# Head maxima and their reciprocals by VectorE's 32x32 block transposes instead of TensorE transposes

## The reference

```python
c = jax.lax.stop_gradient(jnp.max(log_x.real, axis=-1, keepdims=True))
x = jnp.exp(log_x - c + 2).real.reshape(Bsz, L, n * d)
y = jnp.matmul(x, C) + jnp.matmul(u, D)
```

## Time and profile before

| | |
|---|---|
| runs of the kernel before | 208.19, 209.32, 211.12 us; median 209.32 |
| span of the profiled execution | 206.2 us (the page gives no other time of that execution) |
| busy: PE, PE weight loads, DVE, ACT, POOL | 181.0, 163.3, 143.2, 116.5, 97.5 us |
| mean granted clock of PE | 0.991 |

### The profile page before, as it was taken

The page is one execution under the profiler, slowest core; times in us unless marked ns, Lnnn a source line. Parts: engine busy times, 40 slices in busy tenths (PEclk is TensorE's granted clock), DMA queues, the critical chain, the costliest instruction groups (busy, mean ns, idle before and its releaser), DMA issues. The chain is left out here.

```text
span 206.2 us, 4072 instructions
## 1 busy us (share of the span) xinstructions
PE 181.0 (88%) x1407; PEld 163.3 (79%) x1407; DVE 143.2 (69%) x411; ACT 116.5 (56%) x317; POOL 97.5 (47%) x144
## 2 busy tenths in 40 slices
PE   0498999999999999999694999988979979996993
PEld 0276789999899987887594898987969969995891
DVE  1859956753444434669587685995977959569994
ACT  2037986554433355454444577847759577693771
POOL 0116644999200002239576184672843917656441
PEclk9999999999999999999999699999999999999999
DMA  5991000000000000000000000010100100010012
GB/s 137 399 423 62 3 0 5 2 0 3 0 0 3 0 0 2 3 0 0 0 3 2 0 3 0 0 51 5 51 0 3 52 0 27 27 51 2 3 52 102
DMA packets 2566, 7.60 MB, mean 37 GB/s; under 512 B 309, under 2 KB 1122, under 8 KB 2290
## 3 DMA queue, kind: packets, MB, share of 16 engines
q1 hardware_dynamic: 2258, 7.15, 9.1%
q10 hardware_dynamic: 288, 0.20, 0.4%
HBM read 5.25 MB, written 2.10 MB: 36 GB/s over the span
## 5 line engine op out<-in xcount | busy, mean ns | idle before, releaser
L421 POOL TENSOR_TENSOR hid_p<-hid_f,hid_p 128x256 fp32r<-128x256 f32 x56 | 40.2, 734 | 35.8 <-ACT hid_p L566 27.6
L564 ACT ACTIVATE hid_f<-bank,pa 128x256 f32<-128x256 f32 x64 | 30.3, 478 | 22.6 <-PE bank L1091 22.6
L1091 PE MATMUL bank<-xaT_p,fc_p 128*128 128x256 f32 x192 | 35.7, 297 | 0.8 <-ACT hid_f L564 0.7
L1111 PE MATMUL bank<-hid_p,out_hi 128*128 128x256 f32 x128 | 33.6, 288 | 0.6 <-POOL hid_p L421 0.5
L473 ACT ACTIVATE X<-bank 128x128 f32<-128x128 f32 x64 | 17.6, 279 | 23.3 <-PE bank L935 23.1
L1091 PEld LDWEIGHTS bank<-xaT_p,fc_p 128*128 128x128 f32 x192 | 27.3, 191 | 3.4 <-issue 2.0
L932 PE MATMUL bank<-uT,pa 128*128 128x128 f32 x128 | 25.1, 280 | 0.1
L843 DVE TENSOR_SCALAR xp<-h,mv,rstd 128x128 f32<-128x128 f32 x32 | 22.5, 762 | 3.3 <-POOL rstd L439 3.3
L1111 PEld LDWEIGHTS bank<-hid_p,out_hi 128*128 128x128 f32 x128 | 23.8, 188 | 1.2 <-POOL hid_p L421 0.9
L935 PE MATMUL bank<-X,pa 128*128 128x128 f32 x120 | 23.2, 275 | 0.0
L566 ACT ACTIVATE hid_p<-bank,pa 128x256 fp32r<-128x256 f32 x48 | 23.0, 478 | 0.0
(11 more groups left out here) (123 smaller groups left out, 384.4 us busy)
## 6 DMA issues: line engine op xcount, KB each, us to landing
fc_w<-in_fc SPq DMA_DIRECT2D x2, 2048.0 KB, 11.2
out<-res SPq DMA_DIRECT2D x7, 256.0 KB, 2.0
pb<-in_pack_b SPq DMA_DIRECT2D x1, 320.0 KB, 4.2
pa<-in_pack_a SPq DMA_DIRECT2D x1, 279.0 KB, 3.5
out<-res SPq DMA_DIRECT2D x2, 128.0 KB, 1.7
conv_w<-in_conv ACTq DMA_DIRECT2D x1, 128.0 KB, 3.4
pc<-in_pack_c ACTq DMA_DIRECT2D x1, 66.5 KB, 3.8
rowsel<-in_rows SPq DMA_DIRECT2D x1, 64.0 KB, 3.8
```

The costliest lines, as they stand in the source:

```text
L421: nc.gpsimd.tensor_tensor(hid_p[1][:, half, c, :], hid_f[:, m % HID_SLOTS, :], hid_p[0][:, half, c, :].bitcast(F32), ALU.subtract).then_in ...
L564: full = nc.scalar.activation(hid_f[:, m % HID_SLOTS, :], src, ACT.Gelu, bias=bias)
L1091: last = mm(bank[5 + n % 2][:, 0:HALF], fc1_p[w][:, e * HID + c * P:e * HID + (c + 1) * P], xaT_p[m][:, b % 2, half, :], start=(k == 0), s ...
L1111: last = mm(out_bank(b, half)[:, half * HALF:(half + 1) * HALF], out_p[w][:, e, c * CH:(c + 1) * CH], hid_p[m][:, half, c, :], start=(c == ...
```

## The change

The maxima come from X itself: a reduce which transposes each 32x32 block (32 states of a quadrant of partitions by 32 chunks) as it reads, so that chunk k is on a partition of the same quadrant and the reduce runs over 32 states. As a head has 64 states, in two quadrants, PE swaps the quadrants of each pair by one matmul with a permutation matrix, and DVE takes the larger of its own and the swapped value (peak). Reciprocals follow, and two block transposes of a broadcast spread them back to the states' partitions in banks 0 and 1. The factor e squared moves into the product xh. The transposes of X and of r_s on PE, ACT's four copies, the spreading matmuls, the sel matrix with its load and its cast on POOL go. On DVE peak, reciprocal and block transposes stand where xh stands, behind the small rows L801; only the reduces stay at the old place.

```diff
-PC_COLS = dict(ident=P, iota=1, tile=NQ)
+PC_COLS = dict(ident=P, iota=1, swap=P)
...
-        amax = sb("amax", [P, 2, NQ, NH])
-        rcp = sb("rcp", [P, 2, NQ * NH])
-        r_s = sb("r_s", [P, 2, NS, NQ * NH])
-        r_T = sb("r_T", [NS * NQ * NH, 2, L], F32R)
+        amax = sb("amax", [P, 2, NP, T])
+        peak = sb("peak", [P, NP, T])
+        rcp = sb("rcp", [P, NP, T])
...
-        bank_rt = bank[4][0:NS * NQ * NH, 0:P]
+        bank_sw = bank[4][:, 0:NP * T]
...
-                sp.dma_start(sel_f[:], sel).then_inc(ld_sel, 16)
...
-                pool.wait_ge(ld_sel, 16)
-                nc.gpsimd.tensor_copy(sel_r[:], sel_f[:]).then_inc(sel_ready, 1)
...
-                        b = j + 3
-                        if n == 2 and b < NB:
-                            act.wait_ge(rt_done, b + 1)
-                            if b >= 2:
-                                act.wait_ge(R_done, 2 * (b - 1))
-
-                            for q in range(NQ):
-                                mask = pc[0:NS * NQ * NH, PC["tile"]][:, q:q + 1]
-                                last = nc.scalar.activation(r_T[:, b % 2, q * P:(q + 1) * P], bank_rt, ACT.Copy,
-                                                            scale=mask)
-                            last.then_inc(rT_ready, 1)
...
                     b = j + 3
                     if b < NB:
+                        g, bb = divmod(b, GB)
+                        dve.wait_ge(x2_ready[g], T)
+                        if b >= 2:
+                            dve.wait_ge(swap_done, b - 1)
                         for a in range(NP):
-                            dve.wait_ge(xt_done, 2 * b + a + 1)
-                            last = nc.vector.tensor_reduce(
-                                amax[:, b % 2, :, 2 * a:2 * a + 2],
-                                bank[a][:].rearrange("p (q n d) -> p q n d", q=NQ, n=2), AX.X, ALU.max,
-                                apply_absolute_value=True)
+                            last = nc.vector.tensor_reduce(amax[:, b % 2, a, :], X[:, g, a * GB + bb, :, :], AX.X, ALU.max,
+                                                           apply_absolute_value=True, apply_transpose=True)
                         last.then_inc(amax_ready, 1)
-                        dve.wait_ge(amax_ready, b + 1)
-
-                        chained(nc.vector.reciprocal(rcp[:, b % 2, :],
-                                                     amax[:, b % 2, :, :].rearrange("p q n -> p (q n)")))
-                        if b >= 2:
-                            dve.wait_ge(rt_done, b - 1)
-                        hi = r_s[:, b % 2, 0, :]
-                        chained(nc.vector.tensor_scalar(hi.bitcast(F32R), rcp[:, b % 2, :], E2, None, ALU.mult))
-                        nc.vector.scalar_tensor_tensor(out=r_s[:, b % 2, 1, :], in0=rcp[:, b % 2, :], scalar=E2,
-                                                       in1=hi, op0=ALU.mult, op1=ALU.subtract).then_inc(rs_ready, 1)
...
                         if b == 0:
                             dve.wait_ge(fc1_split, NE)
+                        dve.wait_ge(amax_ready, b + 1)
+                        dve.wait_ge(swap_done, b + 1)
+                        nc.vector.tensor_tensor(peak[:], amax[:, b % 2], bank_sw.rearrange("p (a i) -> p a i", a=NP),
+                                                ALU.max).then_inc(peak_ready, 1)
+                        dve.wait_ge(peak_ready, b + 1)
+                        chained(nc.vector.reciprocal(rcp[:], peak[:]))
                         for a in range(NP):
-                            dve.wait_ge(R_done, 2 * b + a + 1)
-                            if b >= 2:
-                                dve.wait_ge(y_done, b - 1)
-                            nc.vector.tensor_tensor(xh[:, b % 2, a, :],
-                                                    X[:, g, a * GB + bb, :, :].rearrange("p i k -> p (i k)"),
-                                                    bank[a][:], ALU.mult).then_inc(xh_ready, 1)
+                            last = nc.vector.transpose(bank[a][:].rearrange("p (i k) -> p i k", k=NCH),
+                                                       rcp[:, a, :].unsqueeze(2).broadcast_to([P, T, NCH]))
+                        chained(last)
+                        if b >= 2:
+                            dve.wait_ge(y_done, b - 1)
+                        for a in range(NP):
+                            nc.vector.scalar_tensor_tensor(
+                                out=xh[:, b % 2, a, :], in0=X[:, g, a * GB + bb, :, :].rearrange("p i k -> p (i k)"),
+                                scalar=E2, in1=bank[a][:], op0=ALU.mult, op1=ALU.mult).then_inc(xh_ready, 1)
...
                         if e == FUSED_FRONT:
                             pe.wait_ge(x2_ready[0], T)
-                            pe.wait_ge(rT_ready, 1)
+                            pe.wait_ge(peak_ready, 1)
...
-                def transpose_r(b):
-                    pe.wait_ge(rs_ready, b + 1)
+                def swap_quadrants(b):
+                    pe.wait_ge(amax_ready, b + 1)
...
-                    nc.tensor.transpose(bank_rt, r_s[:, b % 2, :, :].rearrange("p s n -> p (s n)"),
-                                        ident).then_inc(rt_done, 1)
-
-                def spread_r(b):
...
+                    mm(bank_sw, pc[:, PC["swap"]], amax[:, b % 2].rearrange("p a i -> p (a i)"), start=True,
+                       stop=True).then_inc(swap_done, 1)
...
                 def transpose_h(b):
                     pe.wait_ge(h2_ready, b + 1)
-                    pe.wait_ge(rT_ready, min(b + 2, NB))
+                    pe.wait_ge(peak_ready, min(b + 2, NB))
...
                     scaled, mixed, attended = j + 3, j + 2, j + 1
-                    if scaled < NB:
-                        transpose_x(scaled)
...
                     if scaled < NB:
-                        transpose_r(scaled)
+                        swap_quadrants(scaled)
...
-                    if scaled < NB:
-                        spread_r(scaled)
```

More of the change, by code:

```diff
@@ L91, with build @@
 PC, PC_N = spans(PC_COLS)
-def build(nc, ids, rows, emb, conv, pack_a, pack_b, pack_c, sel, fc1, fc2, out):
+def build(nc, ids, rows, emb, conv, pack_a, pack_b, pack_c, fc1, fc2, out):
     with ExitStack() as ctx:
@@ L105, in build @@
         pb = sb("pb", [P, PB_N])
-        sel_r = sb("sel_r", [NS * NQ * NH, NP * P], F32R)
         fc1_p = [sb(f"fc1_p{s}", [P, NE * HID], F32R) for s in range(NS)]
@@ L216, in build @@
         ks_copied, full_ready = sem("ks_copied"), sem("full_ready")
-        xt_done, amax_ready, rs_ready = sem("xt_done"), sem("amax_ready"), sem("rs_ready")
-        rt_done, rT_ready, R_done, xh_ready = sem("rt_done"), sem("rT_ready"), sem("R_done"), sem("xh_ready")
+        amax_ready, swap_done, peak_ready, xh_ready = (
+            sem("amax_ready"), sem("swap_done"), sem("peak_ready"), sem("xh_ready"))
         y_done, h2_ready, st2_ready, mv2_ready = sem("y_done"), sem("h2_ready"), sem("st2_ready"), sem("mv2_ready")
@@ L1018, in transpose_r @@
                         pe.wait_ge(xa_ready, b - 1)
-                    nc.tensor.transpose(bank_rt, r_s[:, b % 2, :, :].rearrange("p s n -> p (s n)"),
-                                        ident).then_inc(rt_done, 1)
-                def spread_r(b):
-                    pe.wait_ge(rT_ready, b + 1)
-                    pe.wait_ge(sel_ready, 1)
-                    pe.wait_ge(amax_ready, b + 1)
-                    for a in range(NP):
-                        mm(bank[a][:], sel_r[:, a * P:(a + 1) * P], r_T[:, b % 2, :], start=True,
-                           stop=True).then_inc(R_done, 1)
+                    mm(bank_sw, pc[:, PC["swap"]], amax[:, b % 2].rearrange("p a i -> p (a i)"), start=True,
+                       stop=True).then_inc(swap_done, 1)
                 def mixer_out(b, q):
@@ L1193 @@
     pack_b = np.concatenate([parts[n] for n in PB_COLS], 1)
-    tile = np.zeros((P, NQ), np.float32)
-    rows = tile[:NS * NQ * NH].reshape(NS, NQ, NH, NQ)
-    sel = np.zeros((NS, NQ, NH, NP, 2, DH), np.float32)
-    for q in range(NQ):
-        rows[:, q, :, q] = 1
-    for n in range(NH):
-        sel[:, :, n, n // 2, n % 2, :] = 1
-    pack_c = np.concatenate([np.eye(P, dtype=np.float32), np.arange(P, dtype=np.float32)[:, None], tile], 1)
+    eye = np.eye(P, dtype=np.float32)
+    swap = eye.reshape(2, 2, P // 4, P)[:, ::-1].reshape(P, P)
+    pack_c = np.concatenate([eye, np.arange(P, dtype=np.float32)[:, None], swap], 1)
     arrays = dict(
         ids=ids, emb=f(L0_tok_emb_weight), conv=f(L0_tok_conv_weight)[:, 0, :].T.reshape(1, 2 * CH),
-        pack_a=pack_a, pack_b=pack_b, sel=sel.reshape(NS * NQ * NH, NP * P),
+        pack_a=pack_a, pack_b=pack_b,
         pack_c=pack_c, rows=np.repeat(np.eye(2 * NB, dtype=ml_dtypes.bfloat16), P, 1),
```

16 lines of the change are left out of this document (2 added, 14 removed).

## The result

The changed kernel takes 217.78 us (median of four runs, 214.84 to 218.75) against 209.47 us of the kernel before beside it (208.19 to 211.12): a ratio of 1.035, interval 1.027 to 1.043. All ratios here are formed from the faster, undisturbed runs alone (of the changed kernel 214.84 and 217.49 us), so they are not the quotients of the medians. It is slower, as forecast, but the loss is 3.5% and not 1.5%, and the time lies just above the range given (217.0). The profiled execution took 217.49 us with a span of 215.7, so 1.8 us lie around the span; the span grew by 9.5 us where 3.05 were forecast. The forecast of the time had put 3.1 us around the span, so the time was missed by 5.4 us and the span by 6.45.

A forecast was written before the change was run, and what follows sets the result against it. DVE's gapless string was taken to bound the loop, not PE. Terms -1.45 + 2.8 + 1.0 + 0.7 gave +3.05 us, span 209.25; with 3.1 around it 212.4 us, 1.5% slower, range 206.5 to 217.

The forecast's parts named there:

- DVE's string: Batch loop: DVE's gapless instructions set the round, PE has slack; period from 13.57 to 14.1 us, +0.55.
- the prices of what no row had shown: DVE's new instructions: peak 0.19, reciprocal 0.31, two block transposes 1.28 and 0.04, reduces as today; swap on PE 0.2 us.
- Rival C: DVE's transposing instructions run at half rate: four instructions, 0.53 us more each, seven rounds, +15, 227 us; chance 0.10.
- the waits at the swap and at transpose_h: PE in each loop round: some 2.1 us standing for the swap, about 1.2 for peak at transpose_h, free in the loop.
- the stretches without a fall: Sums by part of the span: -2.1 us at j=-1, -1.45 to j=0, +2.8 for four periods, +1.0 after j=4.
- the tail behind j=4: After the last scaling, where PE was the bound: xa ready at 7.6 us after xh's old place against 6.6, +1.0 us.
- the forecast's 2.8: Four periods from j=0 to j=4: +1.05 for the first, +0.65 for the next, two of +0.55, in all +2.8 us.
- One more fall at 0.7: PE's granted clock: waits of 2 to 3 us for the swap bring one further fall, +0.7 us.
- Rival B: The clock falls in every round: five links at 0.7 to 1.1 us each, 215.2 to 217 us; chance 0.15.
- Rival A: xp (L843) leaves POOL's burst of subtractions: up to 1.6 us a period less, about 206.4 us; chance 0.13.

The follow-up runs named there:

- the fillers: The changed kernel with twelve transposes of the identity, result never read, on PE ahead of the swaps of batches 2 to 7; 213.77 us, ratio 1.026.
- the first experiment's kernel: The changed kernel with peak, reciprocal and block transposes moved behind the reduces, ahead of DVE's wait for xaT_p; 203.59 us, ratio 0.975.

## Why the prediction was right or wrong

**Right: DVE's string is the loop, and PE is not the bound.** Duplicated PE work left the time as it was, the string moved into DVE's wait took 1.96 us out of the period, and in a round without a fall DVE stood only before xaT_p.

**Right: the prices of what no row had shown.** Peak 0.18 (0.19 forecast), reciprocal 0.35 (0.31), block transposes 1.32 (1.32), reduces 1.29 (1.28), xh 1.28, swap reached 0.06 us behind the reduces (0.05). Rival C, transposing instructions at half rate, is out.

**Right: the waits at the swap and at transpose_h**, 2.5 and 0.9 us (2.1 and 1.2). What the first did to the clock stands below.

**Right: the stretches without a fall.** -1.76 at j=-2 (-1.85) and again -1.76 at j=-1 (-2.1), the tail behind j=4 at +1.08 (+1.0). The tail is in part luck: up to the small row of j=5 it was +1.49, with res at 1.28 once more, and behind it -0.41, and the forecast did not have the two apart.

**Wrong: the term of res, which the sum put at nothing.** In the period, 13.57 - 1.24 + 1.85 + 0.1 - 0.15 = 14.1, everything behind the string but xp was carried over unchanged. The working followed the string's delay against POOL's burst for xp, which was inside it already, and not for res, which was just ahead of it. It went from 0.68 to 1.28, +0.55 to the period as it overlaps its neighbours. Measured against 14.64: res +0.55, the link from the reduces to xaT_p 2.42 against 2.3, +0.12, the string +0.11, xp 2.39 and not 2.67, -0.28; that is 14.1 + 0.5. Over four periods a loss of 4.2 us (0.99, 1.05, 1.07, 1.07) stood for the forecast's 2.8. In the first of the four the xaT_p wait and L769's stretch differ, so they are not equal terms.

**Wrong in size: the clock.** One more fall at 0.7 was taken; there were two more, at 1.16 and 0.92, and the one in the round to j=0, which both kernels have, cost more than before: 15.07 us for that period where 13.70 and +0.65 had been the sum, as DVE's wait for xaT_p was 3.33 and not 2.45. The longer idle time of PE (3.28 us and not 2.80) doesn't explain it: with the fillers PE stood 1.96 us there, and the period was 15.07 again, while the run with the doubled block transposes, which had no fall there, had a wait of 2.41. What differs is where the fall lies: by the windows 0.5 us behind the start of the swap after the change (0.73 in the window from 114), and 1.0 us behind that of L1019 before it:

```profile
113.00:114.00 1.00, 1.00 (x10) 1.00 (x9) 0.00 (x0) 0.95 (x4) 0.00 (x0) 0.76 0.00 0
```

Rival B (215.2 to 217) was the nearer one by its number, with three falls in six rounds and not one in each; it had no price for res, which lost about as much as the two falls.

**The start.** In the profiled executions it added 2.55 us by the moment at which the embedding's matmuls went from 1.9 to 1.06 us a group, which differs as much between executions of kernels that are the same up to there. It was no term of the forecast, and no experiment ties it to the edit.

**Sum.** 3.05 forecast; +2.55 start; +1.06 to j=0; +1.38 in the clean parts of the four periods; +1.38 for two falls in place of one; +0.08 tail: 9.5. Of the 6.45 us missed 2.76 lie in the four periods and are res and two falls, and 1.06 lie ahead of them: 0.7 with the costlier fall in the round to j=0, and 0.34 up to j=-1, most of it in the round from j=-2, where the forecast had a gain of 0.25 and the period was 13.90 us in both kernels; for that part no run gives the cause. 2.55 is the start.

**Rival A** (xp leaves the burst) did not come: xp was 2.39, still stretched, though a quarter of the way.

## What to carry to other kernels

When a string of instructions is put into an engine's stream, follow every instruction behind it to its new place against the other engines' bursts, not only those that are stretched already: here the one that had been just ahead of the burst paid the most. A string that must be added belongs where that engine waits; against the old kernel the same instructions lost 1.07 us a round at one place and gained 0.89 at the other. Before work is taken from a TensorE that is not the bound, see whether its idle time comes in one piece: here two added falls of its clock cost 2.1 us.

## What the runs showed of the hardware that was not expected

- Falls of the granted clock to 0.50 came behind idle times of 1.86 us (the run with res ahead of peak, 128.77) to 3.7 us before the swap, while others of 1.85 us, 1.86 (the change, 129.16), 2.02 (the swap in bank 1, 176.43) and 2.47 us (the change, 159.60) were without one. So the length of the single idle time doesn't decide it alone. A fall cost 0.9 to 1.2 us in the change and in the first experiment's kernel, and 2.4 where the whole link from the swap to xaT_p ran at 1.2 GHz.
- PE ran at the slow rate for the first 14 to 22 us of an execution, over two to four groups of matmuls (the last of them in part), and differently between kernels that are the same up to there; it moved the last group by 2.8 us, while the granted clock was given as 1.00.
- A wait of 0.9 us in mid-round, with nothing behind it in a hurry, helped to keep the clock up: without it two falls came back and the kernel lost 5.9 us, part of it through xp.
- POOL's power instruction (1.64 us) did not stretch res, whether res started inside it (the kernel before, 0.69 at 159.77) or just ahead of it (the run with res ahead of peak, 0.69); in all four rounds of the latter it was the power that took longer, 2.01 to 2.04 us. The subtractions did stretch res, to 1.28.
- The reciprocal costs by its columns: 0.25 us for 16, 0.35 for 32.
